# Expert loop: VectorE copies a step's result out of PSUM one iteration later, behind the next weight copies

## The reference, cut to what matters

```python
shared_out = _swiglu(x, shared_gate_w, shared_up_w, shared_down_w)
logits = x @ gate_w
topk_ids = jnp.argmax(logits, axis=-1)
...
g = _grouped_mm(sorted_x, routed_gate_w, tokens_per_expert)
u = _grouped_mm(sorted_x, routed_up_w, tokens_per_expert)
d = _grouped_mm(jax.nn.silu(g) * u, routed_down_w, tokens_per_expert)
return (shared_out + routed_out).reshape(b, s, h)
```

## Time and profile before

| | before |
|---|---|
| median of 3 runs | 676.03 us |
| lowest to highest run | 674.29 to 678.47 us |
| span of the profiled execution | 674.0 us |
| TensorE busy | 585.9 us (87%) |
| VectorE busy | 516.2 us (77%) |
| ScalarE busy | 368.2 us (55%) |
| GpSimd busy | 300.5 us (45%) |
| expert loop, first gate/up to the last store's issue | 612.58 to 670.45 us |

### The profile page before, as it was taken

How to read it: one execution, slowest core, us unless ns; L and a number is a source line. 1 busy time by engine, 2 the same in 40 slices (tenths; PEclk the granted TensorE clock), 3 DMA queues, 4 the chain that set the end, 5 groups by cost and what they waited for, 6 DMA issues and landing times.

```text
span 674.0 us, 14407 instructions
## 1 busy us (share of the span) xinstructions
PE 585.9 (87%) x5382; PEld 341.8 (51%) x5382; DVE 516.2 (77%) x919; ACT 368.2 (55%) x586; POOL 300.5 (45%) x254
## 2 busy tenths in 40 slices
PE   3577887999999999999999888878999999878994
PEld 2235655656767657667566556433232334444441
DVE  6787988889788888887898745897777757566772
ACT  0235353567576675765665573414756577436772
POOL 3465464554545554555656433413200010442776
PEclk9979999999999999999999899987999999999998
DMA  8303010010101010101110034344792343115441
GB/s 273 77 16 120 17 34 9 18 33 10 33 17 26 18 25 18 27 15 24 27 26 18 17 94 110 77 71 93 200 232 103 130 156 109 68 36 115 59 53 9
DMA packets 33297, 44.03 MB, mean 65 GB/s; under 512 B 9248, under 2 KB 24652, under 8 KB 32460
## 3 DMA queue, kind: packets, MB, share of 16 engines
q1 hardware_dynamic: 29260, 40.99, 23.0%
q0 software_dynamic: 3968, 2.12, 2.5%
HBM read 27.54 MB, written 8.41 MB: 53 GB/s over the span
## 4 chain that ended last, share of the span: by engine, by line
PE 50%; DVE 25%; issue 12%; ACT 7%; POOL 3%; DMA 2%; POOLq 0%; another core or an unknown queue 0%; DVEq 0%; SPq 0%; ACTq 0%
PE ps L1601 5%; PE ps L1632 4%; PE ps L1823 3%; PE ps L1610 3%; DVE smx L1089 3%; PE ps L1737 3%; DVE ssum L1059 3%; DVE mneg L1291 2%; ACT region_r L895 2%; PE ps L1487 2%; PE ps L1554 2%; PE ps L1502 2%; PE ps L1721 2%; PE ps L1488 2%; PE ps L1573 2%
## 5 line engine op out<-in xcount | busy, mean ns | idle before, releaser
L659 POOL TENSOR_TENSOR rnorm<-ssum_c,neg_half 128x16 f32<-128x16 f32 x32 | 94.8, 2962 | 102.5 <-DVE ssum_c L1062 101.1
L667 POOL TENSOR_TENSOR region_r<-region_b,region_w 128x512 f32<-128x512 f32 x60 | 77.8, 1316 | 43.9 <-DVE region_b L1067 43.4
L1291 DVE TENSOR_REDUCE mneg<-ps 128x2 f32<-128x1024 f32 x64 | 77.2, 1220 | 18.7 <-PE ps L1721 17.6
L895 ACT ACTIVATE region_r<-ps 128x1024 f32<-128x1024 f32 x64 | 63.2, 1024 | 34.2 <-PE ps L1737 34.1
L788 ACT ACTIVATE region_w<-ps 128x1024 f32<-128x1024 f32 x32 | 32.8, 1026 | 53.3 <-PE ps L1488 51.9
L764 ACT ACT_TABLE_LOAD x39 | 50.0, 1283 | 1.4 <-PEq L1970 0.7
L1487 PE MATMUL ps<-region_w,hT 128*128 128x512 f32 x64 | 36.9, 660 | 15.1 <-DVE region_b L1067 14.2
L624 POOL TENSOR_TENSOR var_eps<-mv,eps 128x4 f32<-128x4 f32 x20 | 4.5, 223 | 100.6 <-DVE mv L1004 100.6
L751 POOL DMA_INDIRECT out<-region_r x24 | 37.7, 1571 | 24.4 <-DMA out<-xr 11.3
L1601 PE MATMUL ps<-region_w 128*114 128x512 f32 x96 | 47.2, 615 | 0.6 <-ACT region_w L805 0.6
L1067 DVE TENSOR_TENSOR region_b<-ps,rnorm 128x1024 f32<-128x1024 f32 x32 | 39.1, 1223 | 8.1 <-POOL rnorm L659 7.1
(11 more groups left out here) (287 smaller groups left out, 1413.5 us busy)
## 6 DMA issues: line engine op xcount, KB each, us to landing
region_w<-in_wx SPq DMA_DIRECT2D x16, 768.0 KB, 4.4
region_b<-region_w SPq DMA_DIRECT2D x56, 130.0 KB, 2.3
parts_dram<-region_b SPq DMA_DIRECT2D x6, 384.0 KB, 2.6
xs_dram<-region_w SPq DMA_DIRECT2D x1, 1548.0 KB, 7.6
region_w<-in_wqkv SPq DMA_DIRECT2D x2, 768.0 KB, 8.4
pts<-xs_dram SPq DMA_DIRECT2D x24, 64.0 KB
region_w<-parts_dram SPq DMA_DIRECT2D x3, 384.0 KB, 6.9
region_b<-parts_dram SPq DMA_DIRECT2D x3, 384.0 KB, 7.4
```

What stands on the lines that cost most here:

```text
L659: g.tensor_tensor(rnorm[:, :], ssum_c[n % 2][:, :], neg_half[:, :], ALU.pow).then_inc(S["rnormed"], 1)
L667: g.tensor_tensor(dst, src, tab, ALU.mult).then_inc(S["rot_bb"], 1)
L895: act_(dst, bank(l1_bank[what, b, i], of=2), ACT.Exp).then_inc(T["ex"], 1)
L1291: d.tensor_reduce(mneg[b % 2][:, 2 * i:2 * i + 2], bank(l1_bank[what, b, i], of=2) .rearrange("p (q t) -> p q t", q=2), AX.X, ALU.max, neg ...
```

## The change

In VectorE's loop the copy of a step's result leaves the end of its iteration. It stands in the next iteration, behind that iteration's weight copies and ahead of its gated product; the last step's copy follows the loop. No other engine's code is touched.

```diff
@@ -1425,11 +1425,13 @@
                     weights_one(j + 3, pair)
                 if j + 4 < PAIRS:
                     pair = [expert_of(j + 4, 1)]
+                if j > 0:
+                    routed_sb(j - 1)
                 if j + 2 < PAIRS:
                     gated(j + 2)
                 if j + 4 < PAIRS:
                     pair.append(expert_of(j + 4, 2))
-                routed_sb(j)
+            routed_sb(PAIRS - 1)
```

## The result

| | before | after |
|---|---|---|
| median of 20 runs | 676.51 us | 671.85 us |
| lowest to highest run | 674.01 to 678.95 us | 669.37 to 677.57 us |
| span of the profiled execution | 674.0 us | 670.4 us |
| first gate/up group to start of the last store, in the trace | 56.31 us | 51.27 us |

The ratio is 0.9934, with a 95% interval of 0.992 to 0.9947: 0.66% or about 4.5 us less (3.6 to 5.4), within 1%. The prediction said 671.8 us, 4.3 less than the median of the first three runs.

The account below looks back on a forecast made before the run. Nearly full TensorE, held up by a two-iteration circle through VectorE's queue, was taken as the bound. TensorE's 4.7 us less 0.4 kept by GpSimd gave 4.3 off 676.0, stated as 671.8 us, range 669.0 to 675.5.

Parts of the forecast that it names:

- The circle opens: Loop: weight copies no longer queue behind the waiting result copy; TensorE takes 1.93 us an iteration, not 2.159; 4.1 us.
- VectorE holds it: VectorE's loop: its own circle takes 1.90 us, within TensorE's 1.93; weights are ready 0.25 us before wanted.
- rival B: VectorE becomes the bound, about 2.05 us an iteration; 2.2 us won, 673.8 us; chance 0.21.
- Who waits for the later copy: Moved result copy: comes 3.3 us after gate/up starts, down projection's signal at 2.89, so the copy doesn't wait.
- The start: Loop start: gate/up 5 comes 1.93 us after gate/up 4, 0.6 earlier; gate/up 23 4.7 us earlier.
- The end: GpSimd's last four stores queue at 1.87 us each; the last comes at 664.6, 4.3 us earlier.
- C: TensorE itself makes the gap ahead of gate/up, so early weights win nothing; 676 us; chance 0.10.
- D: Result copy's wait, now ahead of the product, holds product and weights; 5.6 us more, 681.6 us; chance 0.03.
- E: VectorE's weight pairs and GpSimd's stores exclude each other; 7.8 us more, 683.8 us; chance 0.03.
- F: Results come early enough for GpSimd never to wait; 6.2 us won, 669.8 us; chance 0.06.

Follow-up runs that it names:

- e8: The change, with each result copied out of PSUM twice, once into a buffer nobody reads; 671.23 us.
- e1: The kernel before, in its old order, with GpSimd's 24 stores of the expert rows left out; 664.65 us (0.9857 of before).
- e3: Against the kernel before, the result copy one iteration late but left at the end of the iteration, behind the product; 671.4 us (0.9964).
- e6: Second run of the result copy one iteration late at the end of the iteration, beside the change; 671.96 us (0.9947 of before).
- e2: The change's order with GpSimd's same 24 stores left out; 663.9 us (0.9844 of before).
- e9: The change without GpSimd's store of step 10; 672.07 us, beside 676.82 for the kernel before.
- e4: The kernel before, with a GpSimd addition of two 128x512 float32 arrays in place of each store; 678.54 us.
- e7: The kernel before, with SyncE storing each result as a plain DMA into a scratch array in place of GpSimd's indirect store; 665.91 us.

## Why the prediction was right

1. *The circle opens.* Right, in size too: 1.91 us an iteration where I took 1.93 from TensorE's undisturbed one. Over 18 iterations 34.41 us for the 34.74 of the forecast. One reading under it was wrong, without harm: the old chain doesn't pass one gate/up group in every second iteration but all of them; its list of the longest stretches shows only those that begin behind the gap.

2. *VectorE holds it.* Right; product to weight copy is 0.75 as taken, and shrinks to 0.54 when VectorE is late (e8; bound of 0.55). The weight pair was mis-sized: I took 1.14, thinking that GpSimd would be busy beside most pairs. It is, and all but three of the pairs from 619 us on take 0.94 to 0.95 (the others 0.97 to 1.08; behind a further one the copy itself waited 0.18). Even before, most slow pairs took 1.05 or 1.06 until the product. What slowed them down was not any overlap with a store, but one with its last part: the pair of 640.31 began 0.85 behind the start of a store that was being issued for 0.73 more, and the like pairs did so too, while in e8 most begin behind 0.88 to 0.95 of a store, have 0.64 to 0.68 more of it beside them, and take 0.95. That is a reading of positions, not tested. The error was on the cautious side; rival B got its 0.21 from it.

3. *Who waits for the later copy.* Nobody, as forecast. The signal's lateness of 0.77, which I carried over as a constant, was none: by the trace's record of the semaphore it is 0.04 to 0.39 in the change, 0.04 in e1, 0.7 to 1.1 in e3 and e6 and 0.6 to 0.85 in e8 for most steps. It depends on where in a store's issuing the down projection ends. In the change that is mostly 1.2 to 1.34 us into it, near its end, which nobody had aimed at. It cost nothing in any of the late orders, because up to step 19 the copy comes behind the signal, by about 0.9 us or more in the change, e3 and e6, and by 0.4 or more in e8. With 0.77 for a property of TensorE's signal I would have forecast 4.5 us for the change in a kernel without stores, where e1 and e2 show none.

4. *The start.* Gate/up 4 to 5 takes 1.95 instead of 2.52, 0.57 of the 0.6 forecast. In front of it the old trace lost 0.64 us between the first gate/up group and that of step 4, to a token load that landed late (7.34 us against 6.70). That isn't part of the change: e1, in the old order, has 6.72. It is the part of the 5.0 us between the traces that I hadn't forecast.

5. *The end.* From gate/up 4 to the last store: 665.33 - 620.76 = 44.57 us against 48.97 before, 4.40 less, where the sum said 4.3. Store 19 stood 4.58 behind gate/up 21 (I had 4.4; the store follows its copy by 1.35 where I took 1.07), and four stores took 7.45 (7.48).

That the median, 671.85 us, hits the forecast to 0.05 is luck: the interval of the gain is 1.8 us wide, and the two traces differ by 5.0 us, 0.6 of which isn't the change's.

The rivals: B is refuted by e8, C by the groups' distance, D by the result copy's waits (0.2 us between 622 and 657), E by the stores beside the weight pairs, and F by e9 (a missing store wins nothing). E's mechanism exists, though, for another instruction: with additions on GpSimd (e4) it costs 0.64 us an iteration.

## What to carry to other kernels

In an in-order queue, a copy that nobody needs soon but that waits for something can tie two engines into a circle; look for it where the engine that is nearly full has a gap ahead of every second group of its work, and move the copy to where its wait is over. Measure what a wait consists of before costing it: here the engine waited for had been done for 0.77 us, and that was the doing of a third engine. When a loop gets faster, price its end by the queue that drains last.

## What the runs showed of the hardware

- While GpSimd issues an indirect DMA (mostly 1.56 to 1.61 us, at most 1.96), the semaphore signal of a matmul that ends 0.33 to 1.34 us into it arrives 1.23 to 1.50 us behind the start of the issuing (eight traces; step 22 of the change's order is at 0.55). That is up to 1.1 us behind the matmul (e3, e6). It is 0.04 behind the matmul without stores (e1, e2), with additions on GpSimd (e4, three matmuls inside one) and with the same bytes stored by SyncE (e7). The mechanism is open, and whether signals of other engines are held too isn't measured.
- Two 128x768 float32 copies of VectorE take 1.02 to 1.03 us alone (e1, e2) and mostly 1.02 to 1.10 beside a GpSimd store (at most 1.23, e3), and 2.10 beside a GpSimd addition of 128x512, which itself goes from 1.27 to 1.52 (e4).
- A register load from SBUF with its small instructions puts 0.75 us between the start of a 0.42 us product and the next copy when the product had to wait, and 0.54 when it hadn't (e8). No timeline of busy time shows it.
